# Cross-attention and mixture-of-heads kernel: the first batch's key product kept on chip, projection slots re-laid, and two loads issued by ScalarE

## The reference, cut to what matters

```python
# layer 1: cross-attention, 8 heads of 64
q = layernorm(x) @ Wq; k = context @ Wk; v = context @ Wv
x = x + softmax(q k^T / 8) v @ Wo + bo
# layer 2: 16 experts, each with q, k, v, o projections
h = layernorm(x)
rw = gating(h, sim_matrix, gates)            # softmax over the experts that are on
q, k, v = (einsum('bte,bted->btd', rw, einsum('btc,ecd->bted', h, w)) for w in (q_proj, k_proj, v_proj))
a = causal_softmax(q k^T / 8) v
x = x + einsum('bted,edc->btc', a[:, :, None, :] * rw[..., None], o_proj)
```

## Time and profile before

| what | value |
|---|---|
| three runs | 2784.88, 2790.58, 2790.61 us; median 2790.58 |
| the profiled execution | 2798.03 us, its span 2796.2 us |
| busy in that span | PE 2540.1 us (91%), DVE 2163.7 (77%), ACT 1581.0 (57%), POOL 1102.6 (39%) |
| mean granted TensorE clock | 0.966 of full |
| DMA | 445.78 MB, mean 159 GB/s |
| chain that ended last | PE 59%, DMA 14%, DVE 12%, ACT 7%, issue 5% |

### The profile page before, as it was taken

The page is one execution under the profiler, slowest core; times in us unless marked ns, Lnnn a source line. Parts: engine busy times, 40 slices in busy tenths (PEclk is TensorE's granted clock), DMA queues, the critical chain, the costliest instruction groups (busy, mean ns, idle before and its releaser), DMA issues.

```text
span 2796.2 us, 54177 instructions
## 1 busy us (share of the span) xinstructions
PE 2540.1 (91%) x17308; PEld 2455.6 (88%) x17308; DVE 2163.7 (77%) x6107; ACT 1581.0 (57%) x5110; POOL 1102.6 (39%) x1739
## 2 busy tenths in 40 slices
PE   4599999999999999999999998999999998999997
PEld 3488898989898998999899898989899898989896
DVE  4487788778787887878788787878787787878784
ACT  3555555555565555656565565656555555556542
POOL 0134344334344344434344443434434433434442
PEclk7699999999999999999999999999999999999998
DMA  6656545545545545554554554554654554554531
GB/s 166 187 156 188 168 148 172 160 150 157 179 152 167 177 154 164 161 164 143 192 165 148 182 157 141 162 172 135 198 168 147 173 162 148 158 183 157 159 116 42
DMA packets 299938, 445.78 MB, mean 159 GB/s; under 512 B 36856, under 2 KB 210872, under 8 KB 291464
## 3 DMA queue, kind: packets, MB, share of 16 engines
q1 hardware_dynamic: 230024, 374.15, 41.7%
q10 hardware_dynamic: 69632, 68.17, 9.3%
HBM read 257.91 MB, written 184.35 MB: 158 GB/s over the span
## 4 chain that ended last, share of the span: by engine, by line
PE 59%; DMA 14%; DVE 12%; ACT 7%; issue 5%; POOL 1%; SPq 1%; ACTq 0%; DVEq 0%; POOLq 0%
PE bank_b L482 9%; PE bank_b L483 9%; PE bank_b L484 9%; DMA u_dram<-draft 7%; DMA g_dram<-draft 7%; PE bank_c L482 5%; PE bank_c L483 4%; PE bank_c L484 4%; PE bank_a L482 3%; PE bank_a L483 3%; PE bank_a L484 3%; DVE acc L1291 3%; ACT mix L980 2%; PE bank_a L615 2%; DVE mix L1332 2%
## 5 line engine op out<-in xcount | busy, mean ns | idle before, releaser
L1291 DVE SCALAR_TENSOR_TENSOR acc<-bank_b,rw,acc 128x192 f32<-128x192 f32 x1792 | 655.1, 410 | 168.4 <-PE bank_b L484 163.3
L482 PE MATMUL bank_b<-wqkv_hi,x2T_lo 128*128 128x384 f32 (+1 forms) x2048 | 732.2, 358 | 37.5 <-ACT acc L941 37.0
L483 PE MATMUL bank_b<-wqkv_lo,x2T_hi 128*128 128x384 f32 (+1 forms) x2048 | 697.7, 341 | 0.0
L484 PE MATMUL bank_b<-wqkv_hi,x2T_hi 128*128 128x384 f32 (+1 forms) x2048 | 694.0, 339 | 0.0
L911 ACT ACTIVATE probs<-bank_a,s_max 128x77 f32<-128x77 f32 x1024 | 318.5, 327 | 290.3 <-DVE s_max L1224 289.9
L1585 POOL TENSOR_TENSOR mixs_lo<-mix,mixs_hi 128x512 fp32r<-128x512 f32 x256 | 379.3, 1512 | 183.3 <-ACT mixs_hi L1010 183.3
L482 PEld LDWEIGHTS bank_b<-wqkv_hi,x2T_lo 128*128 128x128 f32 x2048 | 389.9, 190 | 52.8 <-ACT acc L941 50.1
L483 PEld LDWEIGHTS bank_b<-wqkv_lo,x2T_hi 128*128 128x128 f32 x2048 | 390.4, 191 | 0.0
L484 PEld LDWEIGHTS bank_b<-wqkv_hi,x2T_hi 128*128 128x128 f32 x2048 | 388.6, 190 | 0.0
L1580 POOL TENSOR_TENSOR probs<-probs,p_sum 128x616 f32<-128x616 f32 x128 | 156.7, 1224 | 365.6 <-DVE p_sum L1231 365.6
L1332 DVE TENSOR_TENSOR mix<-rw_all,late_tiles 128x512 f32<-128x512 f32 x256 | 280.6, 1136 | 18.7 <-ACT late_tiles L1006 18.7
(11 more groups left out here) (204 smaller groups left out, 6398.0 us busy)
## 6 DMA issues: line engine op xcount, KB each, us to landing
g_dram<-draft SPq DMA_DIRECT2D x176, 462.0 KB
gq<-g_dram SPq DMA_DIRECT2D x64, 1232.0 KB, 5.5
uo<-u_dram SPq DMA_DIRECT2D x64, 1024.0 KB
rw_all<-rw_dram ACTq DMA_DIRECT2D x128, 512.0 KB, 7.2
u_dram<-draft SPq DMA_DIRECT2D x176, 308.0 KB
xt<-in_x_dram SPq DMA_DIRECT2D x64, 256.0 KB, 5.0
out_dram<-mix SPq DMA_DIRECT2D x64, 256.0 KB, 4.1
u_dram<-draft SPq DMA_DIRECT2D x88, 156.0 KB
```

The lines of the kernel that those rows point to most:

```text
L482: nc.tensor.matmul(dst, lhs[1], rhs[0], start=start, stop=False)
L483: nc.tensor.matmul(dst, lhs[0], rhs[1], start=False, stop=False)
L484: return nc.tensor.matmul(dst, lhs[0], rhs[0], start=False, stop=stop)
L1291: V.scalar_tensor_tensor(acc[:, t, k, :], src, rw[:, t, e:e + 1], acc[:, t, k, :], ALU.mult, ALU.add).then_inc(b_evac, 1)
```

## The change

- `JOBS` is re-laid: the key and value jobs get places further ahead of the `g` and `u` jobs that use them.
- L1 moves ahead of `b_qkv` 3 and `c_pv` on PE, and correspondingly on ACT and DVE. On PE `b_qkv` 1 moves ahead of M3.
- `load_g` and `load_u` are issued by ACT instead of SP: `load_g` behind the exponentials, `load_u` at the step's end (in a K step, for the next group's first batch, behind the exponentials).
- In the opening, batch 0's part of G is written straight into `gq` by ACT and DVE, and batch 0's part of U goes by DMA from the drafts into `uo`. Only batches 1 and 2 go to DRAM. Transposed x, scores, softmax and output of batch 0 are done inside the opening, step -2 is gone, and there are six drafts there (four of them in `mixs`).
- The small inputs (`sim_matrix`, `gates`, `bo`) load after the first weights, and their work on DVE and PE moves into the opening.

```diff
-    JOBS = ({"E0": ("g", 4), "E1": ("g", 5), "E2": ("v", 0), "E3": ("g", 6), "M1": ("g", 7), "M2": ("u", 0), "L1": ("v", 1),
+    JOBS = ({"E0": ("k", 3), "E1": ("g", 5), "E2": ("v", 0), "E3": ("g", 6), "M1": ("g", 7), "M2": ("v", 1), "L1": ("u", 0),
              "L2": ("u", 1)},
-            {"E0": ("v", 2), "E1": ("u", 2), "E2": ("u", 3), "E3": ("v", 3), "M1": ("u", 4), "M2": ("u", 5), "M3": ("ct", 0),
+            {"E0": ("v", 2), "E1": ("u", 2), "E2": ("u", 3), "E3": ("u", 4), "M1": ("u", 5), "M2": ("v", 3), "M3": ("ct", 0),
              "L1": ("u", 6), "L2": ("u", 7)},
-            {"E0": ("k", 0), "E1": ("g", 0), "E2": ("k", 1), "E3": ("g", 1), "M1": ("g", 2), "M2": ("g", 3), "L1": ("k", 2),
-             "L2": ("k", 3)})
+            {"E0": ("k", 0), "E1": ("k", 1), "E2": ("g", 0), "E3": ("g", 1), "M1": ("g", 2), "M2": ("k", 2), "L1": ("g", 3),
+             "L2": ("g", 4)})
+    OPENING = (("ct", 0), ("k", 0), ("k", 1), ("g", 0), ("g", 1), ("xT", 0), ("k", 2), ("g", 2), ("g", 3), ("k", 3), ("g", 4),
+               ("g", 5), ("v", 0), ("g", 6), ("g", 7), ("s", 0), ("s", 1), ("v", 1), ("s", 2), ("s", 3), ("u", 0), ("u", 1),
+               ("v", 2), ("u", 2), ("u", 3), ("pT", 0), ("pT", 1), ("v", 3), ("pT", 2), ("u", 4), ("u", 5), ("u", 6), ("u", 7),
+               ("ct", 1), ("y", 0))
...
+    FIRST_DRAFTS = 6
...
             for f in range(H):
                 store_g(0, f)
-            load_g(0)
-            load_weights(range(6, 9))
+            load_x(1)
             for f in range(H):
                 store_u(0, f)
-            load_u(0)
-            for i in range(-2, B + 2):
+                if f == 3:
+                    load_weights(range(6, 9))
+            for i in range(-1, B + 2):
                 step(i)
...
+            def first_g(f):
+
+                slot = f % FIRST_DRAFTS
+                if f >= FIRST_DRAFTS:
+                    act.wait_ge(first_out[slot], first_stored(f)[slot])
+                src = bank_job(0, "g", f)[:, 0:2 * KP].rearrange("p (h x) -> p h x", h=2)
+                nc.scalar.activation(gq[:, f // 2, f % 2, 0, :].rearrange("p (h k) -> p h k", h=2), src[:, :, 0:NC], copy)
+                dst = first_drafts[slot][:, 0:GB * 4 * NC].rearrange("p (b l h k) -> p l h b k", b=GB, l=2, h=2)
+                nc.scalar.activation(dst[:, 0, :, 1:GB], src[:, :, NC:KEYS].rearrange("p h (b k) -> p h b k", b=GB - 1), copy).then_inc(g_hi, 1)
...
+            def load_g(n):
+                gm, b = n // GB, n % GB
+                if gm:
+                    for k in range(2):
+                        act.wait_ge(draft_out[k], stored(gm) + 16 * (H // 2))
...
+                act.wait_ge(s_fill, at(2 * NT, n - 1, 3))
+                nc.scalar.dma_start(gq[:, :, :, :, :].rearrange("p a b c d -> p (a b c d)").bitcast(F32), g_dram[gm, b, :, :]).then_inc(g_in, 16)
...
                 do(ahead, a_exp, 3)
+                if i % 3 == 2 and on(i + 1) and i + 1 > 0:
+                    load_u(i + 1)
+                if on(i + 2) and i + 2 > 0:
+                    load_g(i + 2)
...
                 turn("L2")
...
+                if i % 3 != 1 and on(i + 2):
+                    load_u(i + 2)
```

More of the change, by code:

```diff
@@ L103, in job @@
     def job(i, slot):
-        if slot not in JOBS[i % 3]:
+        if slot not in JOBS[i % 3] or i < -1:
             return None
@@ L111, in stored, with u_rows, first_rows, first_stored @@
     def stored(gm):
-        return 16 * (H // 2 + H) * gm
+        return 16 * (H // 2 + H) * (gm - 1)
+    def u_rows(f):
+        k0, k1 = (0, TK) if f % 2 == 0 else (TK, KEYS)
+        return [(b, max(k0 - b * NC, 0), min(k1 - b * NC, NC), max(b * NC - k0, 0)) for b in range(GB)
+                if b * NC < k1 and (b + 1) * NC > k0]
+    def first_rows(f):
+        pieces = []
+        for b, j0, j1, row in u_rows(f):
+            for e in range(2):
+                r = (f // 2 * 2 + e) * NC
+                cuts = [r + j0, *[c for c in range(0, HN, P) if r + j0 < c < r + j1], r + j1]
+                pieces += [(e, row + c0 - cuts[0], c0 // P, c0 % P, c1 - c0) for c0, c1 in zip(cuts, cuts[1:]) if b == 0]
+        return pieces
+    FIRST_DRAFTS = 6
+    first_stores = [1] * H + [len(first_rows(f)) + sum(b > 0 for b, *rest in u_rows(f)) for f in range(H)]
+    def first_stored(before):
+        return [16 * sum(first_stores[s] for s in range(before) if s % FIRST_DRAFTS == k) for k in range(FIRST_DRAFTS)]
     es = ExitStack()
@@ L241, in xattn_moe_kernel @@
         draft_out = [sem(f"draft_out{k}") for k in range(2)]
+        first_out = [sem(f"first_out{k}") for k in range(FIRST_DRAFTS)]
         wq_fill, wq_hi = sem("wq_fill"), sem("wq_hi")
@@ L377, in store_u @@
+                src, out_sem = (draft[:, f % 2, :], draft_out[f % 2]) if gm else (first_drafts[slot], first_out[slot])
                 sp.wait_ge(u_evac, at(H, gm, f))
[L378 to L401, removed]
+                if gm == 0:
+                    for e, row, chunk, p0, count in first_rows(f):
+                        sp.dma_start(uo[p0:p0 + count, chunk, :, :].rearrange("p l c -> p (l c)").bitcast(F32),
+                                     src[row:row + count, e * 2 * C:(e + 1) * 2 * C].bitcast(F32)).then_inc(out_sem, 16)
@@ L749, in _ @@
                     j_g(0, f)
-                else:
-                    j_u(0, f)
+                elif kind == "u":
+                    j_u(0, f)
+                elif kind == "xT":
+                    a_xT(0)
+                elif kind == "s":
+                    a_s(0, f)
+                elif kind == "pT":
+                    a_pT(0, f)
+                else:
+                    a_y(0, 0)
+                    a_y(0, 1)
             def step(i):
-                nxt, ahead, now, before, earlier = [i + d for d in (2, 1, 0, -1, -2)]
+                nxt, ahead, now, before, earlier = i + 2, i + 1 or -1, i, i - 1, i - 2
                 def do(n, fn, *k):
@@ L819, in step @@
                 do(before, c_pT)
+                turn("L1")
                 do(now, b_qkv, 3)
@@ L822, in step @@
                 do(now, b_qkv, 4)
-                turn("L1")
                 do(now, b_qkv, 5)
                 turn("L2")
-            for i in range(-2, B + 2):
+            for i in range(-1, B + 2):
                 step(i)
@@ L1340, in step @@
             def step(i):
-                nxt, ahead, now, before, earlier = [i + d for d in (2, 1, 0, -1, -2)]
+                nxt, ahead, now, before, earlier = i + 2, i + 1 or -1, i, i - 1, i - 2
                 def do(n, fn, *k):
-                    if on(n) and not (fn is ln1_a and n == 0):
+                    if on(n):
                         fn(n, *k)
```

273 lines of the change are left out of this document (183 added, 90 removed).

## The result

| | before | changed |
|---|---|---|
| median (lowest to highest) | 2790.6 us (2779.91 to 2791.17, 6 runs) | 2809.65 us (2804.48 to 2820.73, 6 runs) |
| profiled execution | 2798.03 us | 2807.19 us |
| mean granted clock | 0.966 | 0.954 |
| K/V window, mean of 19 | 45.53 us | 40.96 us |
| V/U window | 38.93 | 39.02 |

The ratio is 1.0068 (95% interval 1.0044 to 1.0093): slower by 0.7%, more than the 0.2% that a measurement can tell. 2807 us was forecast. A step period is the time between two output additions on DVE (line 1437 of the changed kernel), worked out over the steady part from the trace. One window got 4.6 us shorter, another 5.0 us longer, and the third stayed.

What follows compares the result with a forecast made beforehand. PE, busy 91%, was taken as the bound, so its idle time lengthens the run. Steady +27 and opening -11 gave +16 on the profiled 2798.0, or 2807 us as median; likeliest case 2797 to 2850, 8 in 10 2715 to 2865.

Steps and rivals of the forecast that it cites:

- The K/V boundary: Between K and V step: g job 4's wait for a key job's evacuation goes, -3.7 us a group.
- M1 in the K step: ACT's wait at M1 for g0's store: it ends about when it did, 0 us, between -2.5 and +1.5.
- Rival 1: Queues served in turn, so stores overtake loads: 2660 us, or 2727 in half measure; together chance 0.25.
- M1 in the U step: u5, moved to M1, waits for u3's store ahead of xT and c_qk: +5.0 us a group, between +1 and +8.
- what ACT waits at M1, PE waits less 1.1 us: Relation read from K steps: PE's wait at c_s equals ACT's wait at M1 less 1.1 us.
- c_s waits of 0.45 us in U steps: Sign that the forecast is wrong: PE's c_s wait stays 0.45 us in U steps; then the sum's sign turns.
- Why u3's store is late: U step: G's later load pushes u3's store, +0.5 us; by the skill's rule its 38-row half uses two engines.
- ACT's issues: Up to three new DMA issues a step on ACT: 0, at worst +0.6 us a group.
- The steady sum: Steady part: -3.7 + 0 + 5.0 = +1.3 us a group, over 21 groups +27 us.
- The opening: Before the steady part: step 0's first maximum at 114 instead of 125.3, -11 us, bounds -30 and +5.
- The second: Rival: gains and losses balance, the U step's M1 costing only +3; 2770 to 2796 us, chance 0.2.
- The fourth: Rival: the opening gains nothing since y 0 waits for u7's stores; +11, 2818 us, inside the forecast's case.

Runs made afterwards that it cites:

- experiment 2: Changed kernel with the loads of G and U issued by SP again, at their earlier places: 2788.92 us, ratio 0.9999 to the kernel before.
- experiment 1: Changed kernel with the U step's slots as before (v3 at E3, u4 at M1, u5 at M2): 2709.11 us, ratio 0.971 to the kernel before.
- experiment 4: Changed kernel with the 38-row half of each odd U store cut into 32 and 6 rows: 2769.18 us, ratio 0.9929 to the kernel before.
- experiment 9: Changed kernel with the 38-row half of each odd U store cut into 19 and 19 rows: 2921.6 us, ratio 1.0481 to the kernel before.
- experiment 10: Changed kernel with old U slots, k2 at M1, g2 at M2, 32 + 6 row cut, weight pieces 6 to 8 loaded later, loads on ACT: 2611.82 us.
- experiment 3: Changed kernel with key job 2 at M1 and g2 at M2 in the K step: 2744.72 us, ratio 0.9847 to the kernel before.
- experiment 8: Changed kernel with old U slots, k2 at M1, g2 at M2, loads on SP, 32 + 6 row cut, weight pieces 6 to 8 loaded later: 2611.09 us.

## Why the prediction was right, point by point

- **The K/V boundary, -3.7 us a group.** The mechanism was right, and the size nearly: the wait of g 4 is gone, and cut at PE's last product the window lost 3.4 us. Of these 2.4 are idle time of PE (5.4 to 2.9), and 1.0 is busy time, about half of it by the granted clock (0.953 to 0.962 in these windows), where the text had 1.25 for the clock. The 4.6 us between output additions hold the moved edge as well.
- **M1 in the K step, 0.** The size was right: the wait at c_s went from 2.2 to 2.7 us in a K/V window. The reason held in part. g0's store was issued a slot later and landed 2.6 us faster (7.84 instead of 10.44), no longer right behind the loads, and what it shares the engines with is `rw_all`. The reading of the earlier trace rows, that queued work is finished first, stood against the Trainium skill ("DMA: Bandwidth & Descriptors", Queues, rings and completion order) and its turns between queues. The changed kernel's trace shows both again: 4 packets of SP's queue against 79 of ACT's from 582 to 584, and 694 against 998 from 584 to 590. Rival 1, which went by the turns, would have come out at 2660 us; neither g0's nor u3's store gained from the other queue (experiment 2).
- **M1 in the U step, +5.0.** This is the term that was mis-sized. Cut at PE's last product the U/K window grew by 3.9 us, not 5.0: 2.2 us more idle time of PE (1.7 to 4.0 us) and 1.7 more busy time at a granted clock of 0.96 instead of 1.00, against some 3.7 and 1.25 in the text. The relation "what ACT waits at M1, PE waits less 1.1 us" did not carry over from the K step: ACT waited 5.44 us and PE 3.08. The place was wrong too. PE waits at the context job (L564, 3.1 us a step over 21 steps), which the text named only in passing, and at c_s 0.5 us, not 4 to 5. "c_s waits of 0.45 us in U steps" was the text's own sign of being wrong, with the sum's sign to turn; it came, and the sign did not turn, since the wait stood at L564. Taken by itself the new row does cost 5.0 us a group (experiment 1), because the rest of the change had made the U/K window 1.1 us shorter (40.1 to 39.0 at PE's last product): the later fill's wait of 1.06 us a step is 0.06 without the row too.
- **Why u3's store is late.** The text named the load of G, and in a sentence of its own the form. The form costs 0.7 us of 9.7; the bytes beside it are those of `rw_all`, not of G (experiment 4). The Trainium skill (same page, Why a DMA increments its semaphore by 16 and not by 1) has the rule for the form, and the update counts of experiments 4 and 9 agree with it. The text's "no reordering of queues shortens it" held.
- **ACT's issues, 0.** 0 in experiment 10. In the changed kernel the loads on SP gave 20 us, which the landing times of g0's and u3's stores do not explain and which show in good part as a higher clock in the K/V windows. Whether they come from ACT's issues stays open.
- **The steady sum, +1.3 x 21 = +27 us.** Measured +0.5 a group and +10 us from the first output addition to the last. The terms measured are -3.4, +0.1 and +3.9: the U step's was 1.1 us too large, the K/V boundary's 0.3.
- **The opening, -11 us.** Step 0's first maximum came 7.5 us earlier, at 117.8 and not 114. Two errors partly offset: Y's end was put near 87 and was 96.8 (start of its evacuation on DVE, behind SP's loads of weight pieces 6 to 8, which the text did not count among what SP issues ahead of u4's store), and step -1 then took 21 us from there, not 27. The start gained 7.3 us (19.36 to 12.06 for the first key product) instead of 5.5. At the first output addition only 1.1 us was left, in part because of the wait for the last weight piece in step 1, which the text did not have.
- **The sum.** +27 - 11 = +16 was forecast and +19 measured between medians (+9 between the profiled executions). Two misses, 17 us less in the steady part and 4 to 10 us less won in the opening, had opposite signs and partly cancelled, and the profile of before lies 7.5 us above its median, that of the changed kernel 2.5 below. That 2807 lies within 3 us of the median is in part luck. The sign rested on the U step's term, which was too large but held.
- **Rivals.** The second, a balance within 2770 to 2796, is what the profiled steady part nearly shows (+0.5 a group), and its +3 for the U step is about as near the measured +3.9 as the forecast's +5. It was not slack in the step, though: by experiment 1 the row costs 5.0 us for a wait of 5.5 on ACT. The fourth, that the opening gains nothing, is nearly the measured 1.1 us at the first output addition, yet for another reason: step 0 came 7.5 us sooner, and step 1, with its wait for the last weight piece, gave most of it back.

## What to carry to other kernels

Before a job is moved one slot forward, ask which store it must wait for and what stands behind it on the same engine: the same store, equally late, cost nothing behind c_qk and 100 us ahead of it, and the wait showed on PE at a third job that only shared the bank. Where a table of slots decides, try one row at a time: here the U step's row was worth +100 us, the rest of the change -80 us, and one swap of two jobs that the change did not make another -65 us. And cut a transfer by its row count before cutting it by its bytes.

## What was unexpected of the hardware

- Cutting a transfer can make it slower. u5's store (77 rows and the half of 38, of 4 KB each), for which few others compete, lands in 6.16 us, with the half as 32 + 6 in 4.02, as 19 + 19 in 9.58. Two transfers of 19 rows take 3.4 us longer than one of 38 that has two engines; that is as if both had gone to the same engine, one behind the other. The trace names no engine, so this is read from the times alone.
- Idle time on PE costs more than itself. Against the changed kernel, over a whole group of three steps, 2.3 us less idle time won 3.4 us (experiment 3), 3.3 us won 4.5 (experiment 1) and 6.0 us won 9.0 (experiment 8), while 4.5 us more cost 5.5 (experiment 9). The granted clock of most of the windows shown that hold such a wait is 0.92 to 0.96, and it is 1.00 in the stretch of experiment 8 where hardly any such wait is left.
